# Three attentions of sixteen heads: a written table of steps, last keys as 32x32 products, routing in single steps between

## What is computed

```python
x = x + tanh(g_xattn[0]) * L0_xattn(layernorm(x), ctx)   # 16 heads of 16, masked
x = x + tanh(g_ffn[0])   * L0_ffn(layernorm(x))          # coupling net, three rounds
x = x + tanh(g_xattn[1]) * L1_xattn(layernorm(x), ctx)   # 8 heads of 64
x = x + tanh(g_ffn[1])   * L1_ffn(layernorm(x))          # quantised MLP
x = x + tanh(g_xattn[2]) * L2_xattn(layernorm(x), ctx)   # 16 heads of 16, with biases
x = x + tanh(g_ffn[2])   * L2_ffn(layernorm(x))          # 2 of 8 experts for each token
x = x + tanh(g_xattn[3]) * L3_xattn(layernorm(x), ctx)   # 16 heads, unit queries and keys, post-layernorm
x = x + tanh(g_ffn[3])   * L3_ffn(layernorm(x))          # 2 of 16 experts, capacity 320, and a shared expert
```

## Time and profile before

| | us |
|---|---|
| median of 3 runs | 1521.21 |
| lowest, highest | 1521.18, 1521.71 |
| the profiled execution, its own time | 1527.34 |
| its span in the trace | 1525.6 |
| PE busy | 1317.1 (86%) |
| DVE busy | 700.3 (46%) |
| ACT busy | 475.3 (31%) |
| POOL busy | 290.9 (19%) |

### The profile page before, as it was taken

How to read it: one execution, slowest core, us unless ns; L and a number is a source line. 1 busy time by engine, 2 the same in 40 slices (tenths; PEclk the granted TensorE clock), 3 DMA queues, 4 the chain that set the end, 5 groups by cost and what they waited for, 6 DMA issues and landing times.

```text
span 1525.6 us, 18646 instructions
## 1 busy us (share of the span) xinstructions
PE 1317.1 (86%) x6561; PEld 813.4 (53%) x6561; DVE 700.3 (46%) x1985; ACT 475.3 (31%) x891; POOL 290.9 (19%) x381
## 2 busy tenths in 40 slices
PE   5999979959999954899989789994799867999997
PEld 2545444334565641654544579993444445666664
DVE  5755363384356348675554622223535573222114
ACT  1144524411212227114434023331454311222220
POOL 5200010023000001222022422222342224222220
PEclk9699989969999988779989679996798788999999
DMA  9990010010000010000000567764000023344425
GB/s 256 274 295 11 1 52 0 0 56 0 1 0 1 1 32 0 2 18 1 1 29 29 177 194 214 213 194 154 1 0 22 25 68 119 115 161 138 138 86 172
DMA packets 106330, 124.00 MB, mean 81 GB/s; under 512 B 15394, under 2 KB 90782, under 8 KB 106238
## 3 DMA queue, kind: packets, MB, share of 16 engines
q1 hardware_dynamic: 99246, 103.92, 23.5%
q0 software_dynamic: 6992, 18.88, 3.3%
HBM read 73.92 MB, written 48.86 MB: 80 GB/s over the span
## 4 chain that ended last, share of the span: by engine, by line
PE 77%; DVE 10%; issue 4%; ACT 3%; POOL 3%; DMA 1%; SPq 1%; DVEq 0%; POOLq 0%; ACTq 0%
PE bank L1148 9%; PE bank L1182 5%; PE bank L812 5%; PE bank L738 5%; PE bank L1224 4%; PE bank L1191 4%; PE bank L721 4%; PE bank L832 4%; PE bank L1003 3%; PE bank L861 3%; PE bank L850 3%; PE bank L679 2%; PE bank L864 2%; PE bank L913 2%; POOL x_slots L1644 2%
## 5 line engine op out<-in xcount | busy, mean ns | idle before, releaser
L1295 ACT ACTIVATE scratch<-bank 128x512 f32<-128x512 f32 x240 | 126.4, 604 | 98.1 <-PE bank L839 43.7
L1148 PE MATMUL bank<-scratch 128*128 128x320 f32 (+3 forms) x480 | 152.7, 475 | 0.6 <-issue 0.6
L1971 DVE TENSOR_REDUCE scratch<-bank 128x2 f32<-128x308 f32 x256 | 105.5, 472 | 76.5 <-PE bank L812 76.0
L1617 POOL TENSOR_SCALAR rstd<-mv 128x4 f32<-128x4 f32 x36 | 10.0, 278 | 649.7 <-DVE mv L1751 627.9
L1148 PEld LDWEIGHTS bank<-scratch 128*128 128x128 f32 (+1 forms) x480 | 86.7, 184 | 60.3 <-issue 29.2
L2478 DVE TENSOR_TENSOR scratch<-scratch,bank 128x320 f32<-128x320 f32 (+3 forms) x60 | 31.3, 525 | 176.9 <-PE bank L1148 176.9
L1264 ACT ACTIVATE scratch<-bank 128x512 f32<-128x512 f32 x56 | 32.1, 597 | 218.2 <-PE bank L679 218.1
L679 PE MATMUL bank<-ident,scratch 128*128 128x128 f32 x224 | 42.9, 355 | 55.5 <-DVE scratch L1757 37.1
L1644 POOL DMA_INDIRECT x_slots<-scratch x64 | 66.3, 1037 | 110.2 <-DVEq L2335 92.4
L832 PE MATMUL bank<-scratch 32*128 32x512 f32 x384 | 84.8, 668 | 0.6 <-issue 0.5
L812 PE MATMUL bank<-scratch 32*128 32x308 f32 x512 | 83.1, 535 | 1.3 <-DVEq L1830 1.3
(11 more groups left out here) (377 smaller groups left out, 2295.6 us busy)
## 6 DMA issues: line engine op xcount, KB each, us to landing
scratch<-in_L_ffn_W SPq DMA_DIRECT2D x47, 512.0 KB, 4.0
x_slots<-zeros SPq DMA_DIRECT2D x1, 17680.0 KB, 74.3
scratch<-y_back SPq DMA_DIRECT2D x16, 512.0 KB, 8.0
scratch<-in_L_ffn_w_gate SPq DMA_DIRECT2D x16, 352.0 KB, 3.0
scratch<-in_L_ffn_w_up SPq DMA_DIRECT2D x16, 352.0 KB, 3.7
x_slots<-zeros SPq DMA_DIRECT2D x1, 5200.0 KB, 92.3
scratch<-x_slots SPq DMA_DIRECT2D x39, 130.0 KB, 3.1
y_back<-zeros SPq DMA_DIRECT2D x1, 4352.0 KB, 39.8
```

The source lines that it names most:

```text
L1148: last = pe.matmul(bk[0:fn, 0:n], w[s][:, k, m * P:m * P + fn], moving(k), start=k == 0, stop=k == DK - 1)
L1295: act.activation(v["PT"][:, n % 2, j, :], bk[:], ACT.Exp, scale=float(v["hd"]) ** -0.5).then_inc(RP.read, 1)
L1971: dve.tensor_reduce(v["mx"][:, TPC * c + t, r, 2 * m:2 * m + 2], bk[:, 0:2 * M].rearrange("p (e k) -> p e k", k=M), AX.X, ALU.max)\
```

## The change

`steps16` no longer builds its list by rules but reads it from three tables for each attention: FIRST (before the first chunk), EACH (gone through for c = -1 to 3, a step that names chunk c + n being taken where this chunk exists) and LAST. Steps change their places against each other on all engines.

- "rem" is one step for each chunk: sixteen products of 32 rows by 32 columns (two instructions each), four into each of four banks. Product j of group g reads rows 32j on and writes partitions 32(j ^ g) on. In L0 and L2 sixteen products with the maxima follow, of the same form in bfloat16. ACT takes the four exponentials into a buffer of its own, `PR`. `Kr` is a plain copy of the last keys (one POOL instruction in place of four), and `Vr` is laid out for the new places: DVE writes it in six instructions in place of four for each batch.
- "rest" is gone: chunks 2 and 3 have "stats" and "normal" steps, as all others in L3.
- "next G" is split: DVE's part is "next gates", and stands earlier than PE's transposes.
- The bias row is added chunk by chunk after "normal" (`add_bias`), and each "tail" (L2) or "post" (L3) waits for its chunk.
- "ahead keys turned" takes banks of RP, and ACT spreads the keys in place of DVE. POOL's copy of the last keys comes last of all in L2.
- In L2 `tile_table` no longer reads the bank: the counts are taken in `slots`.
- A buffer (`ye`) of L3's experts moves.

The core of the diff:

```diff
+        FIRST = {
+            0: [
+                ("values", 0, 0), ("yT", 0), ("keys", 0), ("proj", 0), ("max", 0, 0, 0), ("max", 0, 1, 0),
+                ("max", 0, 2, 0), ("yT", 1), ("max", 0, 3, 0), ("max", 0, 0, 1), ("max", 0, 1, 1), ("max", 0, 2, 1),
+                ("max", 0, 3, 1), ("values", 0, 1), ("negm", 0), ("proj", 1)],
+            2: [
+                ("yT", 0), ("keys", 0), ("proj", 0), ("max", 0, 0, 0), ("yT", 1), ("max", 0, 1, 0),
+                ("max", 0, 2, 0), ("max", 0, 3, 0), ("max", 0, 0, 1), ("max", 0, 1, 1), ("max", 0, 2, 1),
+                ("max", 0, 3, 1), ("values", 0, 1), ("negm", 0), ("values", 0, 0), ("proj", 1)],
+            3: [
+                ("combine", 0), ("stats", 0), ("normal", 0), ("yT", 0), ("combine", 1), ("stats", 1), ("proj", 0),
+                ("normal", 1), ("unit", 0), ("turn", 0)]}
...
+            2: [
+                ("stats", 3), ("scores", 0, 0), ("norm", -1, 2), ("av", -1, 3), ("normal", 2), ("max", 1, 0, 0),
+                ("rem", 0), ("next b2", -3), ("max", 1, 0, 1), ("next scatter", -3), ("next yT", -2), ("av", 0, 0),
+                ("max", 1, 1, 0), ("scores", 0, 1), ("max", 1, 1, 1), ("norm", -1, 3), ("yT", 2), ("next lg", -2),
+                ("max", 1, 2, 0), ("turn back", -1), ("max", 1, 2, 1), ("av", 0, 1), ("max", 1, 3, 0),
+                ("scores", 0, 2), ("max", 1, 3, 1), ("next top", -2), ("proj", 2), ("tail", -1), ("next gates", -2),
+                ("negm", 1), ("next stats", -1), ("scores", 0, 3), ("norm", 0, 0), ("av", 0, 2), ("next G", -2),
+                ("next normal", -1), ("next pos", -2), ("norm", 0, 1)],
+            3: [
+                ("yT", 1), ("norm", -1, 2), ("scores", 0, 0), ("combine", 2), ("next normal", -2), ("next pos", -3),
+                ("av", -1, 3), ("rem", 0), ("stats", 2), ("norm", -1, 3), ("av", 0, 0), ("next yT", -2),
+                ("next res", -3), ("scores", 0, 1), ("next lg", -2), ("normal", 2), ("turn back", -1), ("proj", 1),
+                ("av", 0, 1), ("next top", -2), ("unit", 1), ("tail", -1), ("next scatter", -3), ("combine", 4),
+                ("scores", 0, 2), ("norm", 0, 0), ("norm", 0, 1), ("post", -1), ("next stats", -1),
+                ("scores", 0, 3), ("av", 0, 2), ("turn", 1)]}
...
+            2: [
+                ("av", 3, 3), ("next yT", 2), ("norm", 3, 2), ("norm", 3, 3), ("next lg", 2), ("next top", 2),
+                ("turn back", 3), ("next scatter", 1), ("ahead keys", 0), ("next gates", 2), ("tail", 3),
+                ("next G", 2), ("next stats", 3), ("next pos", 2), ("next normal", 3), ("ahead values", 0, 0),
+                ("next scatter", 2), ("ahead values", 0, 1), ("next yT", 3), ("next lg", 3), ("next top", 3),
+                ("next pos", 3), ("next gates", 3), ("next b2", 2), ("ahead unit keys", 0), ("next b2", 1),
+                ("next G", 3), ("next b2", 3), ("ahead keys turned", 0), ("next scatter", 3)],
+            3: [
+                ("norm", 3, 2), ("av", 3, 3), ("norm", 3, 3), ("next normal", 2), ("next pos", 1), ("turn back", 3),
+                ("next yT", 2), ("tail", 3), ("next lg", 2), ("post", 3), ("next scatter", 1), ("next up", 0, 0),
+                ("next stats", 3), ("next up", 0, 1), ("next product", 0, 0), ("next top", 2),
+                ("next product", 0, 1), ("next normal", 3), ("next up", 0, 2), ("next up", 1, 0),
+                ("next product", 0, 2), ("next product", 1, 0), ("next pos", 2), ("next up", 1, 1), ("next yT", 3),
+                ("next product", 1, 1), ("next res", 1), ("next lg", 3), ("next top", 3), ("next up", 1, 2),
+                ("next product", 1, 2), ("next pos", 3), ("next res", 3), ("next down", 0), ("next res", 2),
+                ("next scatter", 2), ("next down", 1), ("next scatter", 3)]}
...
                     elif what == "rem":
-                        g = i[0]
-                        m, e = divmod(g, 2)
-                        if g == 0 and c == 0:
+
+                        if c == 0:
                             pe.wait_ge(kr16_made, LA[L] + 1)
-                        bk = RP.take(pe, p, "s", c, g, 4)
+                        pe.wait_ge(RP.read, RP.n(p, "q", c, MT - 1))
                         if has_max:
-                            pe.matmul(bk[:], selxr[:, g, :, :].rearrange("p j k -> p (j k)"), v["negm"][:, c, :],
-                                      start=True, stop=False)
-                        pe.matmul(bk[:], v["Kr"][:, m, b, e, :, :].rearrange("p j k -> p (j k)"), v["QT"][:, c, m, :],
-                                  start=not has_max, stop=True).then_inc(RP.filled, 1)
+                            pe.wait_ge(neg_made, NC * L + c + 1)
+                        bks = []
+                        for g in range(G):
+                            m, e = divmod(g, 2)
+                            bks.append(RP.take(pe, p, "r", c, g))
+                            for j in range(4):
+                                rows, to = slice(32 * j, 32 * (j + 1)), slice(32 * (j ^ g), 32 * (j ^ g) + 32)
+                                last = pe.matmul(bks[g][to, :], v["Kr"][rows, m, b, e, :], v["QT"][rows, c, m, :],
+                                                 start=True, stop=not has_max)
+                            if not has_max:
+                                last.then_inc(RP.filled, 1)
+                        for g in range(G if has_max else 0):
+                            for j in range(4):
+                                rows, to = slice(32 * j, 32 * (j + 1)), slice(32 * (j ^ g), 32 * (j ^ g) + 32)
+                                last = pe.matmul(bks[g][to, :], selxr[rows, g, j, :], v["negm"][rows, c, :],
+                                                 start=False, stop=True)
+                            last.then_inc(RP.filled, 1)
...
+            def add_bias(row, made, n, p, c):
+
+                pool.wait_ge(ln_y, lnorm(p, c))
+                pool.wait_ge(made, n)
+                a = X[:, TPC * c:TPC * (c + 1), :]
+                pool.tensor_tensor(a, a, bc(row.unsqueeze(1), (P, TPC, D)), ALU.add).then_inc(xbias, 1)
```

229 lines of the change are left out of this document (89 added, 140 removed).

## The result

The changed kernel takes 1445.8 us (median; 1443.0 to 1449.8), a ratio of 0.9481 to the kernel before, 95% interval 0.9446 to 0.9515. The prediction was 1457 us, so faster was right and 11 us of the gain were not foreseen. The ratio stands for 1525 us before, not for 1521.2: the kernel before ran again beside each later kernel and then had medians of 1525.3 to 1526.8 us, with single executions from 1517.7 to 1532.1. The profiled execution takes 1445.6 us with a span of 1443.6 us, against 1525.6 before: 82.0 us less. Against the forecast of 64 that is 18 us more, since the profiled execution before was 6.1 us above its median.

A forecast was written before the change was run, and what follows sets the result against it. PE was taken to bound the attention middles by its work, in L3 also by holes and work at 1.2 GHz. Terms sum to -64 us, giving 1457 us against the 1521.2 us median; own range 1430 to 1476, whole range 1430 to 1502.

The forecast's parts named there:

- The terms of the order: Fronts and middles of L0, L2 and L3: moved steps give -4, +3, -5 and -3, -8, -13 us.
- What bounds the kernel: Attention middles: PE's work in L0 and L2; in L3 also holes and 1.2 GHz work, "yT" waits 22.9 us.
- the end of L3: Scatter 1 on POOL ahead of the root of "next stats 3" makes it 4 us late: +4 us.
- The middle of L3: Waits of 7.4 and 9.0 us mostly go, 2 to 3 us of each remain: -13 us (0 to -25).
- The last keys: "rem": sixteen products run at once, 1.4 us a chunk in L0 and L2, 1.1 in L3; 26 and 9 us gained.
- rival A: Whole kernel: order gives nothing or new waits eat its gains, 35 us of "rem" remain: 1480 to 1488 us; 20%.
- rival B: "rem": products pack by four only, losing 9 us in place of gaining 35: 1501 us; 12%.
- rival C: "rem": sixteen products run one by one, as all write banks another row tile is writing: 1635 us; 8%.
- The banks: Ahead of "rem", which takes four banks at once: new waits priced at 0 to 2 us a chunk, none counted.
- Fronts and ends: Chains from engine to engine around the middles: fronts L0 -4, L2 +3, L3 -5 us; ends L2 -4, L3 +4.
- The signs: Profile after: forecast wrong if PE's waits for ACT before "rem" exceed 2 us a chunk, or DVE ends L2's middle waits.

## Why the prediction was right, and where it was not

**The total.** The two halves of the sum were both off, in opposite directions. The terms of the order make 30 us, and the order alone brought 54; the products were put at 35, and brought 25 on top of it. So 1457 against 1446 us is closer than the parts were: 10 of the 24 us by which the order was underrated were cancelled by luck.

**What bounds the kernel.** "PE's own work is the time" held for L0 and L2, "PE's work, plus holes, plus work done at 1.2 GHz" for L3. The next sentence, "Each comes from the order of steps: post, next stats, next normal stand right ahead of the next yT", is only a part of it. The place of "yT" does make a wait (14 us for moving it in the changed kernel), and 12.6 of 18.4 us of these waits remain when it is not touched. But in the kernel before, 11 us hung on another step, at which the sentence does not look: "next scatter" ahead of the roots on POOL. The prediction had just this reading for the end of L3, from the earlier trace rows, and wrote of the DMAs in the body that they stand where POOL is idle. That was said of L2; for L3's body the queue was not looked up. In the changed kernel only one "next scatter" is left in L3's body, and POOL is idle for 5 us behind it.

**The middle of L3.** This is the term that was mis-sized: -13 for the order, measured -27.3 (155.2 to 127.9 with the order alone). It divides by the rows of the stretch into 17.5 us less time without work (25.1 to 7.6) and 9.7 us less busy time (130.06 to 120.33), which goes with the clock of 0.97 in place of 0.85:

```profile
1055.47:1183.41 127.94, 120.33 (x721) 63.95 (x720) 69.87 (x243) 70.43 (x146) 33.64 (x35) 0.97 0.03 9
```

The sum assumed that 2 to 3 us of each wait would remain since VectorE's chain is about as long as PE's work; the wait fell to 0.2 us. And it named the clock but put no number to it. The kernel with filled waits shows that this alone was worth about 8 to 10 us in the kernel before.

**The last keys.** Right in the step itself: 1.5 us a chunk against 1.4 forecast, where no bank is late. The gain of 13 us each in L0 and L2 was 10, in the new order. With waits for banks the step takes 1.8 us on the mean, and four whole products in a row take 4.4 us, not 4.7. PE's timeline of the kernel with the order alone has 4.2 us from the first product on, and ahead of it stands a selector of 0.22 us whose record is missing (12 of 16 are there). Eight times the difference is some 20.5 us, and 20.7 were measured. The lines of that timeline:

```profile
101.50 1.02 PE L841 MATMUL bank<-scratch 128*128 128x512 f32 x2 [0.16 <-ACT scratch L1255]
...
105.68 0.80 PE L799 MATMUL bank<-scratch 32*128 32x308 f32 x8
```

In L3 8.3 came for 9. But for the kernel before, the sum added this term as if it stood by itself, and rival A (only the products count, 1486 us) did the same. By the experiment neither holds: in the old order, with the step placed as in that kernel, the products made the kernel slower by 14 us. That rival was the wrong way round; the order alone brings 54 of 79 us, and it is what lets the products count.

**Rivals B and C.** The sixteen run at once: 0.88 us and 1.5 with the selectors, where rival B had 6.0 with the selectors and rival C 14 for the products. The rule of the Trainium skill, "TensorEngine Tiling (Array Packing)", Gotcha 1, that different row tiles can't use one PSUM bank at the same time, would have made it 14 us a chunk; the trace doesn't agree, with four row tiles in each bank, on different partitions, and 0.88 us for all. The estimate worked out from the Trainium skill, "TensorE: Matmul & The Clock Gate", Part 3, was 1.4 us for this; 0.88 was measured.

**The banks.** "I take none" is the term that was missing in the last keys. "rem" waits for banks in the new order too: 0.3 us a chunk on the mean in L0 and L2, and in L3 it takes 0.7 to 1.3 us more than forecast. All lie in the range of 0 to 2 us that the prediction names. In the old order the products gave nothing in L0 and L2; that waits of this kind ate it is shown for the maxima in part, and argued for the rest.

**Fronts and ends.** The prediction has them all at a clock of 0.57 to 0.79; L3's end was not among its rows, and there the clock was 0.95 with PE busy 39.8 of 49.7 us. L0's front, L2's front and L2's end came within 2 us of the forecast. L3's front gave 9.3 for 5. At L3's end the forecast queue is there: the variances are done at 1171.11, and the root stands behind the scatter:

```profile
1170.73 0.38 DVE L1770 BATCH_NORM_AGGREGATE mv<-stats 128x2 f32<-128x6 f32 x4
...
1175.39 0.96 POOL L1666 DMA_INDIRECT x_slots<-scratch  x1 [0.30 <-issue]
1176.38 0.24 POOL L1639 TENSOR_SCALAR rstd<-mv 128x4 f32<-128x4 f32 x1
...
1192.62 1.93 POOL L1666 DMA_INDIRECT x_slots<-scratch  x1 [0.31 <-DVEq L2358]
```

It is 5.3 us late, but the end is only 1.1 us longer, not 4: POOL issues sixteen DMAs from 1182.13 to 1203.53 with no pause over 0.31 us, so scatter 3 starts as soon as scatter 2 is issued, and the root's delay seems to be covered by that issue. This is read from the timeline; no run moves this scatter. The forecast had the wait and missed its cover.

**The signs.** Of what the profile after was to show, the line of "rem" (1.1 to 1.3 us without waits), the wait of "yT" (0.4 us), the clock in L3 (0.99) and the root behind eight DMAs are there. L0's and L2's middles are 2 and 6 us above what was named, L3's 13 below. One of the two signs that the forecast is wrong came true all the same: DVE ends 5.2 of the 5.9 us of waits in L2's middle, 3.1 of them at one place, the last "tail". It was a poor sign, for in the kernel before DVE ends 6.1 of 9.3 us there.

## What to carry to other kernels

When a wait of the bounding engine ends with a row of another engine, follow it on through every queue on the way, and look at what the queue's engine does right before the releasing instruction, even where it shows no idle time; two scatters of 10 us, each in front of an inverse root of 1.3 us, cost 11 us here. A saving on the bounding engine counts only if the banks behind it come free as fast; try a packed step and the order around it together. When a step is moved in an experiment, look what moves with it: the kernel with the maxima apart got its idle time from "negm". And give a number to the clock: take the busy time of the same instructions at full clock in another stretch, and subtract.

## What the runs showed of the hardware

- Sixteen float32 products of 32x32 by 512 columns on sixteen distinct blocks of the array, with four row blocks writing each bank, take 0.88 us; one product of 128x128 takes 0.95. On four blocks the same sixteen take 3.46.
- Sixteen bf16 products of the same shape take 0.62 us on sixteen blocks and 0.97 on four, where one of 128 rows takes 0.22: they gain far less. What limits them was not tested.
- Useless products can make a kernel faster: 42 of them in three waits gave 0.66%, as the granted clock in the stretch went from 0.85 to 0.96.
- Fillers that run past the wait give the gain back: dummy products expected at 0.21 us each took 0.23 to 0.48, and the stretch from L2's last tail to L3's first "yT" was 4.5 us shorter once 39 of them were taken out. Dummies that write the bank for which PE is waiting start only behind the wait: 14 of them put off the "tail" by 3.2 and 6.0 us.
